# Attention and a block-quantised FFN on one core: up, down and output products cut into half jobs, placed by a table

## The chip, the cores and the metric

The kernel runs on one core of a Trainium2 chip. The metric is the device time of one launch in microseconds. PE is TensorE, DVE VectorE, ACT ScalarE, POOL GpSimd and SP SyncE.

## What is computed

Input x is 4 batches of 1024 tokens of width 128, fp32. xn is its layer norm, and the result is x plus attention of xn plus a gated FFN of xn.

```python
def _L0_attn_ref(inputs, Wq, bq, Wk, bk, Wv, bv, Wo, bo):      # 16 heads of 8
    q = split_heads(inputs @ Wq + bq)                           # k, v alike
    bias = alibi_slopes(H)[:, None, None] * rel                 # rel = key position
    scores = jnp.einsum('bhqd,bhkd->bhqk', q, k) * scale + bias[None]
    attn = jax.nn.softmax(scores, axis=-1)
    ctx = jnp.einsum('bhqk,bhkd->bhqd', attn, v)
    return ctx @ Wo + bo
...
def fp4_linear(x, w):                                           # blocks of 16 on a 4-bit grid
    return jnp.einsum('bsk,nk->bsn', fp4_quant_dequant(x), fp4_quant_dequant(w))
gate = fp4_linear(x, w_gate)                                    # 128 -> 352
y = fp4_linear(x, w_up)
h = jax.nn.silu(gate) * y
return fp4_linear(h, w_down)                                    # 352 -> 128
...
xn = _layernorm(x, axis=-1)
x = x + _L0_attn_ref(xn, ...) + _L0_ffn_ref(xn, ...)
```

## The kernel before

**Attention, in units.** Four heads at a time (a quad), half of the queries (512) at a time, the work goes by blocks of 128 keys: a unit U has four score products (keys x 512 queries, one for each head, L955), four exponentials (L630) and one value product of four heads in column tiles (L966, eight passes), which adds up over the eight units of a half in the bank pv. There are 256 units (NU), 8 to a half and 64 to a batch. The value product of unit U - 1 stands at the end of unit U. The softmax needs each row's maximum first. For that the scores are made once more with queries as rows: a chunk is 128 queries x 1024 keys of one head, in two products (L936), and DVE takes its maximum (L811). Sixteen chunks make a half. Chunks run ahead of the scores by LEAD, which is 22: 22 are done before unit 0, then two in each unit. On PE the products of a chunk and the scores are issued in turn and work on different halves of the rows, a pair at a time. When a half's sixteen maxima are there, DVE writes them in two bf16 parts (L816, L817, called the maximum parts here), PE turns them (job "turn", L944), ACT copies them (L636), and SP writes them to DRAM and back into a row of the queries' operand (L379, L382), two units before the half's first score.

**Jobs.** Everything else is a job that is put into a unit by a formula of its number (`extras`, L99): the FFN goes by pairs of token tiles (16 pairs, one in every 15 units): xT (transposes of the quantised input), gate (two halves, a product of 352 columns each), up (both halves, four passes, L989), hT (two, three transposes each, L997), down (both halves, twelve passes, L1005). The projections of a group of four token tiles are xnT, q, k, v. pvT transposes a finished half of pv (L1016) after ACT has copied it (L667), and DVE divides by the row sums (L841, L842). ctxT and wo (L1029) make the output of a group. All jobs of a unit stand in its middle: on PE after its first chunk and two scores, on ACT after two exponentials, on DVE before the unit's second maximum.

**Two rings of banks.** The first three banks of `low` are a ring for scores and for the jobs that ACT empties (xT, gate, hT, xnT, q, k, v, turn, ctxT, the weights' gT, uT, dT); the two slots of `mx`, two banks each, are a ring for chunks and for what DVE empties (up, down, pvT, wo, bvo). The n-th use of a ring waits until use n - 3 (n - 2 in mx) has been read (`free_bank`, `free_slot`). Each engine works in the order of its own code; semaphores count the uses.

**The quantiser.** After up, DVE multiplies gate and up to hid (L826), takes block maxima of hid and of the next pair's xn (L784, L787), scales and reciprocals (L795 to L798), POOL multiplies (L477, L479), DVE masks exponents (the powers, L804), and POOL rounds by an addition and a subtraction (L489 to L508), from which hT and the next xT are made. POOL also makes the gate's swish (L551), the norm of later groups and the three bf16 parts of q and k.

Of the kernel before, what the change touches and what calls it, by code (L numbers as in the profile page):

```python
# [13 lines left out]
P = 128  # L14
# [3 lines left out]
I = 352  # L18
# [85 lines left out]
def extras(U):  # L104

    out = []
    p, f = divmod(U - ffn_unit(0), ffn_unit(1) - ffn_unit(0))
    if 0 <= p < NP:
        out += {0: [("xT", p)], 1: [("gate", p, 0)], 2: [("gate", p, 1)], 4: [("up", p)], 12: [("hT", p, 0)],
                13: [("hT", p, 1)], 14: [("down", p)]}.get(f, [])  # L110
    for g in range(2, NG):
        if 0 <= U - group_unit(g) < 4:
            out.append((("xnT", "q", "k", "v")[U - group_unit(g)], g))
    out += [("turn", m) for m in range(LEAD // 16, HALVES) if turn_unit(m) == U]
    m, f = U // KT - 1, U % KT
    if m >= 0:
        out += [("pvT", m)] * (f == 2)
        if m // 2 % QUADS == QUADS - 1:
            out += {4: [("ctxT", m // 8 * 2 + m % 2)], 5: [("wo", m // 8 * 2 + m % 2)]}.get(f, [])
    out += {0: [("bvo",)], 7: [("gT",)], 8: [("uT",)], 9: [("dT",)]}.get(U, [])  # L120
    return out


IN_DVE_RING = ("up", "down", "pvT", "wo", "bvo")


def rings():
# [16 lines left out]
    for U in range(NU + KT):  # L144
        for i in range(2):
            if LEAD + 2 * U + i < CHUNKS:
                to_dve("max", LEAD + 2 * U + i)
            for j in (2 * i, 2 * i + 1):
                if U < NU:
                    to_act("exp", U, j)  # L150
            for job in extras(U) if i == 0 else ():
                (to_dve if job[0] in IN_DVE_RING else to_act)(*job)
# [6 lines left out]
def attn_ffn(nc, x, wq, bq, wk, bk, wv, bv, wo, bo, wg, wu, wd, out):  # L159
    with ExitStack() as ctx:  # L160
# [145 lines left out]
        def _(sp):  # L306
# [78 lines left out]
            def store(hb):  # L385
                g, i = hb, hb % 2
                sp.wait_ge(mx_free, MX["wo", hb] + 1)
# [14 lines left out]
            for U in range(NU + KT):  # L402
                for m in range(LEAD // 16, HALVES):
                    if turn_unit(m) + 1 == U:
                        max_rows(m)
                for g in range(2, NG):
                    if group_unit(g) + 8 == U:
                        parts_to_dram(g)
                for b in range(1, B):
                    for quad in range(QUADS):  # L410
                        if max(group_unit(2 * b + 1) + 9, (b - 1) * QUADS * UNITS + (quad + 1) * UNITS + 1) == U:
                            gather(b, quad)
                for job in extras(U - 1):
                    if job[0] == "wo":
# [6 lines left out]
        def _(pool):  # L421
# [136 lines left out]
            for U in range(NU):  # L558
                b, u = divmod(U, QUADS * UNITS)
                if u == 2:  # L560
                    add_bias(b)
                for g in range(2, NG):
                    if U == group_unit(g) - 2:
                        normalize(g)
                    if U == group_unit(g) + 2:
                        three_parts(g, 0, "q")
                    if U == group_unit(g) + 3:
                        three_parts(g, 1, "k")
                for p in range(NP):
                    if U == ffn_unit(p) + 3:  # L570
                        swish(p)
                    if U == ffn_unit(p) + 5:
                        scale_to_grid(p + 1)
                    if U == ffn_unit(p) + 7:
                        round_on_grid(p + 1)
# [3 lines left out]
        def _(act):  # L579
# [57 lines left out]

            std(0)
# [18 lines left out]
            for U in range(NU + KT):  # L657
# [10 lines left out]
                for job in extras(U):  # L668
                    kind, p = job[0], job[1] if len(job) > 1 else 0
                    if kind == "xT":  # L670
                        full("xT", p)
                        if p:
                            act.wait_ge(mx_full, MX["up", p - 1] + 1)
                        nc.scalar.copy(xqT[:], bank("xT", p)[:, 0:PW]).then_inc(st_free, 1)
                    elif kind == "gate":
                        t = job[2]
                        full("gate", p, t)
                        if p:
                            act.wait_ge(mx_free, MX["up", p - 1] + 1)
                        nc.scalar.activation(tanh_s[:, t * I:(t + 1) * I], bank("gate", p, t)[:, 0:I], ACT.Tanh, scale=0.5)  # L680
                        nc.scalar.copy(gate_s[:, t * I:(t + 1) * I], bank("gate", p, t)[:, 0:I]).then_inc(st_free, 1)  # L681
                    elif kind == "hT":
                        t = job[2]
                        full("hT", p, t)
                        if p:
                            act.wait_ge(mx_full, MX["down", p - 1] + 1)
# [418 lines left out]
```

## Time and profile before

| what | value |
|---|---|
| median of 3 runs | 901.21 us (895.38 to 918.01) |
| the profiled execution | 894.07 us |
| its span | 892.3 us |
| PE, DVE, ACT, POOL busy | 87%, 83%, 71%, 39% of the span |
| maxima on DVE (512) | 611.6 us |
| exponentials on ACT (1024) | 552.0 us |
| DMA | 35 GB/s over the span |

The span is from the first to the last instruction of the program; the profiled execution's own time lies 1.8 us above it. In a timeline row stand the start, the duration, the engine, the line, the operation, the tiles (written <- read) with partitions x elements, the number of instructions, and in brackets how long the engine had been idle and for whom it waited. The sum of busy times of one engine says how much work it has; who sets the length of a unit is read from the order of starts.

### The profile page before, as it was taken

To read this page: it belongs to the slowest core of one execution; us is meant where nothing else is said; L and a number is where in the kernel's file an instruction comes from. 1 tells how busy PE (TensorE), PEld (TensorE's weight loads), DVE (VectorE), ACT (ScalarE), POOL (GpSimd) and SP (SyncE) were. 2 spreads that over 40 slices of the span, in tenths; PEclk is the share of its full clock that TensorE was granted. 3 is DMA by queue.
4 is the path that set the end of the run, shared out by engine and by line. 5 is a ranking of instruction groups with operands and counts; after the bars stand their busy time and mean duration, and the time that the engine had idled before them with its cause. 6 is when DMAs were issued, how large, how long until landed. Compare 5 with 4: busy or idle time off the path is not lost.

```text
span 892.3 us, 13552 instructions
## 1 busy us (share of the span) xinstructions
PE 772.9 (87%) x4939; PEld 225.7 (25%) x4939; DVE 741.1 (83%) x878; ACT 633.0 (71%) x1262; POOL 349.3 (39%) x271
## 2 busy tenths in 40 slices
PE   3279989898989989897989989898989898979896
PEld 2012223221223323231323323222213231313222
DVE  7898898889888888978898888989897989898920
ACT  4106878777777878776877778777777687767775
POOL 7272172624226373715053553615152505141320
PEclk9557999999999999999999999999999999999999
DMA  5900020131001020320102020310102000000000
GB/s 156 256 13 2 1 72 3 52 92 36 3 13 37 13 72 2 101 44 1 37 2 49 13 73 1 107 37 1 37 2 49 13 3 1 2 1 2 2 1 24
DMA packets 32826, 31.83 MB, mean 36 GB/s; under 512 B 4344, under 2 KB 26552, under 8 KB 32760
## 3 DMA queue, kind: packets, MB, share of 16 engines
q1 hardware_dynamic: 32760, 30.96, 12.8%
q8 instruction: 40, 0.66, 0.3%
q14 instruction: 26, 0.21, 0.1%
HBM read 15.91 MB, written 15.04 MB: 35 GB/s over the span
## 4 chain that ended last, share of the span: by engine, by line
PE 58%; DVE 27%; ACT 8%; issue 4%; POOL 2%; DMA 1%; SPq 0%; ACTq 0%; DVEq 0%; POOLq 0%
PE low L966 22%; DVE neg_max L811 19%; PE mx L936 18%; ACT probs L630 6%; PE low L955 5%; PE mx L1005 3%; PE mx L989 3%; PE low L983 2%; DVE am L784 1%; DVE mb L804 1%; PE low L922 1%; ACT pv_s L667 1%; PE low L997 1%; DVE hid L826 1%; DVE inv L798 1%
## 5 line engine op out<-in xcount | busy, mean ns | idle before, releaser
L811 DVE TENSOR_REDUCE neg_max<-mx 128x1 f32<-128x1024 f32 x512 | 611.6, 1221 | 91.6 <-PE mx L936 80.2
L630 ACT ACTIVATE probs<-low 128x512 f32<-128x512 f32 x1024 | 552.0, 603 | 182.1 <-PE low L955 180.4
L936 PE MATMUL mx<-k_op,q_op 51*128 51x512 bf16 x1024 | 318.5, 398 | 55.9 <-DVE neg_max L811 33.4
L955 PE MATMUL low<-q_op,k_op 53*128 53x512 bf16 x1024 | 329.0, 389 | 8.0 <-ACT probs L630 2.5
L966 PE MATMUL low<-probs,v_op 128*32 128x512 f32 x2048 | 277.4, 614 | 7.1 <-ACT pv_s L667 5.9
L551 POOL TENSOR_SCALAR tanh_s<-tanh_s 128x704 f32<-128x704 f32 x16 | 31.7, 1982 | 313.7 <-ACT gate_s L681 313.7
L936 PEld LDWEIGHTS mx<-k_op,q_op 51*128 51x128 bf16 x1024 | 62.6, 95 | 358.5 <-DVE neg_max L811 197.2
L955 PEld LDWEIGHTS low<-q_op,k_op 53*128 53x128 bf16 x1024 | 68.5, 94 | 76.5 <-ACT probs L630 63.8
L489 POOL TENSOR_SCALAR mb<-mb 128x960 f32<-128x960 f32 (+2 forms) x17 | 58.8, 3456 | 39.6 <-DVE mb L804 37.9
L966 PEld LDWEIGHTS low<-probs,v_op 128*32 128x32 f32 x2048 | 40.5, 108 | 89.9 <-issue 46.1
L477 POOL TENSOR_TENSOR zb<-hid,inv 128x704 f32<-128x704 f32 x16 | 22.2, 1387 | 97.7 <-DVEq L799 97.7
L491 POOL TENSOR_TENSOR zb<-zb,mb 128x960 f32<-128x960 f32 (+2 forms) x17 | 38.2, 2247 | 1.3
L490 POOL TENSOR_TENSOR zb<-zb,mb 128x960 f32<-128x960 f32 (+2 forms) x17 | 38.2, 2244 | 1.4
L636 ACT COPY max_t<-low 32x128 bf16<-32x128 bf16 x32 | 8.1, 254 | 39.1 <-PE low L944 39.0
L983 PE MATMUL low<-gT_s,xqT 128*128 128x352 f32 x64 | 27.5, 511 | 0.2
L552 POOL TENSOR_TENSOR gate_s<-tanh_s,gate_s 128x704 f32<-128x704 f32 x16 | 27.0, 1686 | 1.3
L944 PE MATMUL low<-ident_b,neg_parts 128*32 128x128 bf16 x32 | 7.2, 224 | 22.4 <-DVE neg_parts L817 19.4
L1005 PE MATMUL mx<-dT_s,hqT 128*128 128x128 f32 (+1 forms) x192 | 25.7, 283 | 0.0
L1016 PE MATMUL mx<-ident,pv_s 128*128 128x128 f32 x128 | 20.2, 280 | 5.0 <-DVE neg_max L811 3.9
L1005 PEld LDWEIGHTS mx<-dT_s,hqT 128*128 128x128 f32 (+1 forms) x192 | 22.6, 191 | 6.8 <-DVE neg_max L811 4.7
L989 PE MATMUL mx<-uT_s,xqT 128*128 128x352 f32 x64 | 23.2, 485 | 0.0
L501 POOL TENSOR_TENSOR hq<-zb,sc 128x704 f32<-128x704 f32 x16 | 22.3, 1392 | 1.3
(120 smaller groups left out, 522.3 us busy)
## 6 DMA issues: line engine op xcount, KB each, us to landing
q_op<-q_rows SPq DMA_DIRECT2D x32, 192.0 KB, 3.8
k_op<-k_rows SPq DMA_DIRECT2D x32, 192.0 KB, 4.7
q_rows<-qp SPq DMA_DIRECT2D x8, 384.0 KB, 2.6
k_rows<-kp SPq DMA_DIRECT2D x8, 384.0 KB, 3.2
x_s<-in_L_attn_inputs_dram SPq DMA_DIRECT2D x8, 256.0 KB, 3.7
q_rows<-qp SPq DMA_DIRECT2D x8, 256.0 KB, 3.1
k_rows<-kp SPq DMA_DIRECT2D x8, 256.0 KB, 3.1
out_dram<-o_s SPq DMA_DIRECT2D x8, 256.0 KB, 2.3
```

The costliest lines, as they stand in the source:

```text
L489: link(nc.gpsimd.tensor_scalar(m, m, 1.0, ROUND, ALU.max, ALU.mult))
L490: link(nc.gpsimd.tensor_tensor(z, z, m, ALU.add))
L491: link(nc.gpsimd.tensor_tensor(z, z, m, ALU.subtract))
L551: link(nc.gpsimd.tensor_scalar(tanh_s[:], tanh_s[:], 1.0, None, ALU.add))
L630: nc.scalar.activation(probs[U % 3][:, 2 * g + x, :], bank("exp", U, j), ACT.Exp).then_inc(st_free, 1)
L811: nc.vector.tensor_reduce(to, slot("max", pos)[:], AX.X, ALU.max, negate=True).then_inc(mx_free, 1)
L936: ins = nc.tensor.matmul(slot("max", pos)[:, 512 * kh:512 * kh + 512], q, k, start=True, stop=True)
L955: nc.tensor.matmul(bank("exp", U, j), k_op[quad][r, g, kt * P:(kt + 1) * P], q_op[quad][r, g, half * HALF:(half + 1) * HALF], start=True, ...
L966: ins = nc.tensor.matmul(pv[32 * hh:32 * hh + 32, :], v_op[b % 2][:, kt, 4 * quad + hh, :], probs[U % 3][:, hh, :], start=(kt == 0), stop= ...
L983: nc.tensor.matmul(bank("gate", p, t)[:, 0:I], xqT[:, t * P:(t + 1) * P], gT_s[:], start=True, stop=True).then_inc(st_full, 1)
L989: ins = nc.tensor.matmul(slot("up", p)[:, 512 * t:512 * t + I], xqT[:, t * P:(t + 1) * P], uT_s[:], start=True, stop=True)
L1005: ins = nc.tensor.matmul(slot("down", p)[:, t * P:(t + 1) * P], hqT[t][0:n, c * P:(c + 1) * P], dT_s[0:n, c * P:(c + 1) * P], start=(c == ...
```

## The change

Up, down and wo, which DVE empties, are cut into two jobs of half the size. `extras` and the formulas of unit numbers go; `plan` builds a table AT at build time. A unit may hold one job in its middle (gate, q, k, v, the weights' transposes and bvo) and one at its end (all others); a job whose place is taken moves to the next unit. At the end means: on PE behind the value product, which now stands right after the unit's last score, on ACT after the fourth exponential, on DVE after the second maximum. ACT's copy of pv moves from behind the second exponential to behind the first. The block maxima are taken inside the second up half's job, the scales after the next unit's first maximum, the reciprocal after its second. LEAD is 23, so a half's last maximum and its parts come one chunk sooner. The gate weights' transposes move from units 7 to 9 to units 1 to 3, and the units of POOL's and SP's work are derived from the table.

```diff
-LEAD = 22
+LEAD = 23
...
-def ffn_unit(p):
-    return 10 + 15 * p
-
-
-def group_unit(g):
-    return 13 + 60 * (g // 2 - 1) + 15 * (g % 2)
+FFN_FIRST, FFN_STEP = 4, 15
+MIDDLE = ("gate", "q", "k", "v", "gT", "uT", "dT", "bvo")
+IN_DVE_RING = ("up", "down", "pvT", "wo", "bvo")
...
+def plan():
+
+    at, busy = {}, set()
+
+    def put(first, *job):
+        place = job[0] in MIDDLE
+        while (first, place) in busy:
+            first += 1
+        busy.add((first, place))
+        at[job] = first
+        return first
+
+    for U, job in enumerate(("bvo", "gT", "uT", "dT")):
+        put(U, job)
+    for m in range(HALVES):
+        if m >= LEAD // 16:
+            put(turn_unit(m), "turn", m)
+        put(KT * (m + 1) + 2, "pvT", m)
+    x_at = put(FFN_FIRST, "xT", 0)
+    for p in range(NP):
+        U = put(x_at + 1, "gate", p, 0)
+        U = put(U + 1, "gate", p, 1)
+        U = put(U + 2, "up", p, 0)
+        up = put(U + 1, "up", p, 1)
+        if p + 1 < NP:
+            x_at = put(max(FFN_FIRST + FFN_STEP * (p + 1), up + 7), "xT", p + 1)
+        U = put(up + 7, "hT", p, 0)
+        U = put(U + 1, "hT", p, 1)
+        U = put(U + 1, "down", p, 0)
+        put(U + 1, "down", p, 1)
...
+    for hb in range(2 * B):
+        U = put(at["pvT", hb // 2 * 8 + 6 + hb % 2] + 1, "ctxT", hb)
+        for i in range(2):
+            U = put(max(U, at["down", 2 * hb + 1, 1]) + 1, "wo", hb, i)
+    return at
...
-                for j in range(2):
+                for j in range(4):
                     exponential(U, j)
-                if U % KT == 1 and U > KT:
-                    m = U // KT - 1
-                    act.wait_ge(pv_done, U - 1)
-                    if m:
-                        act.wait_ge(mx_full, MX["pvT", m - 1] + 1)
-                    nc.scalar.copy(pv_s[:], pv).then_inc(pv_kept, 1)
...
+                    if j == 0 and U % KT == 1 and KT < U <= NU + 1:
+                        m = U // KT - 1
+                        act.wait_ge(pv_done, U - 1)
+                        if m:
+                            act.wait_ge(mx_full, MX["pvT", m - 1] + 1)
+                        nc.scalar.copy(pv_s[:], pv).then_inc(pv_kept, 1)
+                    for job in middle(U) if j == 1 else ():
+                        job_on_scalar(job)
+                for job in end(U):
+                    job_on_scalar(job)
...
+                    mark(nc.vector.scalar_tensor_tensor(hid[:, half], gate_s[:, half], 0.5, slot("up", p, t)[:, 0:I],
+                                                        ALU.mult, ALU.mult))
+                    settle()
                     dve.sem_inc(mx_free, 1)
+                    if t == 1:
+                        block_maxima(p + 1)
...
                     for p in range(NP):
-                        if U == ffn_unit(p) + 5 and i == 0:
-                            block_maxima(p + 1)
-                        if U == ffn_unit(p) + 5 and i == 1:
-                            block_scales(p + 1)
-                        if U == ffn_unit(p) + 7 and i == 0:
+                        if U == AT["up", p, 1] + 1:
+                            (block_scales if i == 0 else block_inverses)(p + 1)
+                        if U == AT["up", p, 1] + 3 and i == 0:
                             powers(p + 1)
+                for job in end(U):
+                    job_on_vector(job)
...
-                    for job in extras(U) if i == 0 else ():
+                    if 0 < U <= NU and i == 1:
+                        value_product(U - 1)
+                    for job in middle(U) if i == 0 else ():
                         job_on_array(job)
-                if 0 < U <= NU:
-                    value_product(U - 1)
+                for job in end(U):
+                    job_on_array(job)
```

On PE, near the down job of the sixth pair. mx<-k_op,q_op is half a chunk, low<-q_op,k_op a score, low<-probs,v_op the value product, mx<-dT_s,hqT down. Before, one unit and its neighbour's value product:

```order
L966 MATMUL low<-probs,v_op 32x512 x4
L936 MATMUL mx<-k_op,q_op 128x512
L955 MATMUL low<-q_op,k_op 128x512
L936 MATMUL mx<-k_op,q_op 128x512
L955 MATMUL low<-q_op,k_op 128x512
L1005 MATMUL mx<-dT_s,hqT 128x128 x6
L936 MATMUL mx<-k_op,q_op 128x512
L955 MATMUL low<-q_op,k_op 128x512
L936 MATMUL mx<-k_op,q_op 128x512
L955 MATMUL low<-q_op,k_op 128x512
L966 MATMUL low<-probs,v_op 32x512 x4
```

And now, from the end of one unit over the next:

```order
L1020 MATMUL low<-probs,v_op 32x512 x4
L1058 MATMUL mx<-dT_s,hqT 128x128 x3
L990 MATMUL mx<-k_op,q_op 128x512
L1009 MATMUL low<-q_op,k_op 128x512
L990 MATMUL mx<-k_op,q_op 128x512
L1009 MATMUL low<-q_op,k_op 128x512
L990 MATMUL mx<-k_op,q_op 128x512
L1009 MATMUL low<-q_op,k_op 128x512
L990 MATMUL mx<-k_op,q_op 128x512
L1009 MATMUL low<-q_op,k_op 128x512
L1020 MATMUL low<-probs,v_op 32x512 x4
L1069 MATMUL mx<-ident,pv_s 128x128 x4
```

Down has left the place between a unit's two chunks; half of it stands behind the value product, and so does pvT one unit later.

On DVE, from the up job of the second pair to the powers. neg_max<-mx is a chunk's maximum, hid the product of gate and up, am the block maxima, sc, scn and inv scales and reciprocal, mb the powers. Before:

```order
L826 SCALAR_TENSOR_TENSOR hid<-gate_s,mx 128x704
L811 TENSOR_REDUCE neg_max<-mx 128x1 x2
L784 TENSOR_REDUCE am<-hid 128x44
L787 TENSOR_REDUCE am<-xn_s 128x16
L811 TENSOR_REDUCE neg_max<-mx 128x1
L795 TENSOR_SCALAR sc<-am 128x60
L796 TENSOR_SCALAR scn<-am 128x60
L798 RECIPROCAL inv<-scn 128x60
L811 TENSOR_REDUCE neg_max<-mx 128x1 x3
L804 TENSOR_SCALAR mb<-zb 128x960
```

And now:

```order
L876 SCALAR_TENSOR_TENSOR hid<-gate_s,mx 128x352
L859 TENSOR_REDUCE neg_max<-mx 128x1 x2
L876 SCALAR_TENSOR_TENSOR hid<-gate_s,mx 128x352
L829 TENSOR_REDUCE am<-hid 128x44
L832 TENSOR_REDUCE am<-xn_s 128x16
L859 TENSOR_REDUCE neg_max<-mx 128x1
L840 TENSOR_SCALAR sc<-am 128x60
L841 TENSOR_SCALAR scn<-am 128x60
L859 TENSOR_REDUCE neg_max<-mx 128x1
L847 RECIPROCAL inv<-scn 128x60
```

The product comes in halves a unit apart, the block maxima stand directly behind the second one, and one maximum stands between the scales and the reciprocal.

## Rows read from the trace of the kernel before

**Rows 1.** The page, busy time of each engine (share of the span) x instructions.
```profile
PE 772.9 (87%) x4939; PEld 225.7 (25%) x4939; DVE 741.1 (83%) x878; ACT 633.0 (71%) x1262; POOL 349.3 (39%) x271
```
**Rows 2.** The page's costliest group: busy, mean ns | idle before, releaser.
```profile
L811 DVE TENSOR_REDUCE neg_max<-mx 128x1 f32<-128x1024 f32 x512 | 611.6, 1221 | 91.6 <-PE mx L936 80.2
```
**Rows 3.** Timeline of PE over a unit without a job: start, duration, what.
```profile
129.02 1.06 PE L966 MATMUL low<-probs,v_op 128*32 128x512 f32 x8
...
131.17 0.39 PE L955 MATMUL low<-q_op,k_op 53*128 53x512 bf16 x1
131.48 1.06 PE L966 MATMUL low<-probs,v_op 128*32 128x512 f32 x8
```
**Rows 4.** Timeline of ACT and of DVE in the same unit.
```profile
130.51 2.06 ACT L630 ACTIVATE probs<-low 128x512 f32<-128x512 f32 x4 [0.39 <-PE low L955]
...
128.20 4.81 DVE L811 TENSOR_REDUCE neg_max<-mx 128x1 f32<-128x1024 f32 x4 [0.31 <-PE mx L936]
```
**Rows 5.** Timeline of PE, a unit with hT in its middle.
```profile
136.34 0.55 PE L997 MATMUL low<-ident,hq 128*128 128x128 f32 x3
136.82 0.39 PE L936 MATMUL mx<-k_op,q_op 51*128 51x512 bf16 x1
```
**Rows 6.** Timeline of PE, a unit with down.
```profile
142.24 1.60 PE L1005 MATMUL mx<-dT_s,hqT 128*128 128x128 f32 x12
143.78 0.39 PE L936 MATMUL mx<-k_op,q_op 51*128 51x512 bf16 x1
```
**Rows 7.** Timeline of PE, the copy of pv and the unit with pvT.
```profile
223.43 1.07 PE L966 MATMUL low<-probs,v_op 128*32 128x512 f32 x8 [0.58 <-ACT pv_s L667]
...
224.96 0.66 PE L1016 MATMUL mx<-ident,pv_s 128*128 128x128 f32 x4
226.35 0.39 PE L936 MATMUL mx<-k_op,q_op 51*128 51x512 bf16 x1 [0.73 <-DVE neg_max L811]
```
**Rows 8.** Timeline of PE, up and q behind each other, then k.
```profile
302.24 1.45 PE L989 MATMUL mx<-uT_s,xqT 128*128 128x352 f32 x4
303.53 1.02 PE L922 MATMUL low<-xnT_s,wq_s 128*128 128x512 f32 x2
...
306.99 1.12 PE L922 MATMUL low<-xnT_s,wk_s 128*128 128x512 f32 x2
308.05 0.39 PE L936 MATMUL mx<-k_op,q_op 51*128 51x512 bf16 x1
```
**Rows 9.** Timeline of DVE after the up of the third pair.
```profile
207.57 0.89 DVE L826 SCALAR_TENSOR_TENSOR hid<-gate_s,mx 128x704 f32<-128x704 f32 x1 [0.22 <-PE mx L989]
...
211.30 0.88 DVE L784 TENSOR_REDUCE am<-hid 128x44 f32<-128x704 f32 x1
...
212.42 1.22 DVE L811 TENSOR_REDUCE neg_max<-mx 128x1 f32<-128x1024 f32 x1
...
214.54 3.49 DVE L811 TENSOR_REDUCE neg_max<-mx 128x1 f32<-128x1024 f32 x3
217.95 0.65 DVE L804 TENSOR_SCALAR mb<-zb 128x960 int32<-128x960 int32 x1
```
**Rows 10.** Timeline of PE, four units behind that up.
```profile
219.79 0.39 PE L936 MATMUL mx<-k_op,q_op 51*128 51x512 bf16 x1 [0.69 <-DVE neg_max L811]
```
**Rows 11.** Timeline of PE, value products 0 and 254 (x256 in all).
```profile
72.24 1.08 PE L966 MATMUL low<-probs,v_op 128*32 128x512 f32 x4
...
881.81 1.06 PE L966 MATMUL low<-probs,v_op 128*32 128x512 f32 x8
```
**Rows 12.** Timeline of DVE and POOL where both work on SBUF.
```profile
417.70 2.19 DVE L817 TENSOR_TENSOR neg_parts<-neg_max,neg_parts 128x16 bf16<-128x16 f32 x1
...
417.66 2.21 POOL L490 TENSOR_TENSOR zb<-zb,mb 128x960 f32<-128x960 f32 x1
```
**Rows 13.** Timeline of SP's queue and of PE, at the start of a half.
```profile
190.41 1.01 SPq L382 DMA_DIRECT2D q_op<-m_rows  x2
...
193.51 0.39 PE L955 MATMUL low<-q_op,k_op 53*128 53x512 bf16 x1
```

More of the change, by code:

```diff
@@ L101 @@
 HEAD = ((1, 0), (1, 1), (0, 0), (0, 1))
[L104 to L121, printed above, removed]
@@ L124, with norm_unit, parts_unit @@
-IN_DVE_RING = ("up", "down", "pvT", "wo", "bvo")
+def norm_unit(b):
+    return 1 if b == 1 else 60 * b - 59
+def parts_unit(g):
+    return 60 * (g // 2 - 1) + 16 + 15 * (g % 2)
+def plan():
[25 more added lines that the diff above has]
+        put(U + 1, "down", p, 1)
+    for b in range(1, B):
+        for g in (2 * b, 2 * b + 1):
+            U = norm_unit(b) + 1 + 8 * (g % 2)
+            for name in ("xnT", "q", "k"):
+                U = put(U + 1, name, g)
+            assert U < parts_unit(g)
+            put(max(U, QUADS * UNITS * (b - 1) + 2) + 1, "v", g)
+    for hb in range(2 * B):
[3 more added lines that the diff above has]
+    return at
@@ L127, in rings, with middle, end @@
+AT = plan()
+JOBS = {}
+for _job, _unit in AT.items():
+    JOBS.setdefault(_unit, []).append(_job)
+def middle(U):
+    return [job for job in JOBS.get(U, ()) if job[0] in MIDDLE]
+def end(U):
+    return [job for job in JOBS.get(U, ()) if job[0] not in MIDDLE]
 def rings():
@@ L143, in rings, with to_ring @@
             to_act("turn", 0)
-    for U in range(NU + KT):
+    def to_ring(job):
+        (to_dve if job[0] in IN_DVE_RING else to_act)(*job)
+    for U in range(NU + 2 * KT):
         for i in range(2):
@@ L401, in _ @@
             max_rows(0)
[L402 to L405, printed above, removed]
+            for U in range(NU + 2 * KT):
+                for job in JOBS.get(U - 1, ()):
+                    if job[0] == "turn":
+                        max_rows(job[1])
                 for g in range(2, NG):
-                    if group_unit(g) + 8 == U:
+                    if parts_unit(g) + 4 == U:
                         parts_to_dram(g)
@@ L655, in _ @@
             keep_turn(0)
[L657 removed]
+            for U in range(NU + 2 * KT):
                 if 3 <= U < NU:
                     act.wait_ge(pv_done, U - 2)
[L660 removed]
+                for j in range(4):
                     exponential(U, j)
[L662 to L711 removed]
@@ L872, in _ @@
             block_scales(0)
+            block_inverses(0)
             for pos in range(LEAD):
@@ L876, in _ @@
                 reduce_chunk(pos)
-            for U in range(NU + KT):
+            for U in range(NU + 2 * KT):
                 for i in range(2):
                     pos = LEAD + 2 * U + i
-                    if i == 1:
-                        for job in extras(U):
-                            job_on_vector(job)
+                    for job in middle(U) if i == 1 else ():
+                        job_on_vector(job)
                     if pos < CHUNKS:
@@ L1065, in _ @@
                     turn(0)
-            for U in range(NU + KT):
+            for U in range(NU + 2 * KT):
                 for i in range(2):
```

161 lines of the change are left out of this document (92 added, 69 removed).

## The prediction

> **What bounds the kernel now.** I read the page's busy line first: PE is busy 87% of the span, DVE 83%, ACT 71%, POOL 39% [rows 1]. The costliest group, the row maxima on DVE, is 611.6 us [rows 2], so DVE is near the end-setter without being it. The averages don't say what ends a unit, so I went to the timeline of one unit without any job. From one value product to the next is 131.48 - 129.02 = 2.46 us [rows 3]. In those 2.46 us the fourth score stands at 131.17, 1.15 us after the unit's first pair (1.00 us behind the value product's start, at 130.02). Low has three banks, so this score takes the bank of the unit's first score, which ACT frees when its first exponential (start 130.51, four of them in 2.06 us [rows 4], so 0.49 apart and about 0.6 long) is done. Then 0.31 us later the value product starts, and it holds PE for 1.00 us. So a clean unit is a loop PE, ACT, PE: 0.49 + 0.60 + 0.06 + 0.31 + 1.00 = 2.46. DVE needs two maxima, 1.14 apart when nothing is missing (four in 4.81 us with 0.1 idle, [rows 4]), 2.28: it has 0.18 to spare in a unit, and a second chunk may come 0.3 us late before it moves the fourth score.
>
> Jobs cost the rest. Value product 0 starts at 72.24 and value product 254 at 881.81 [rows 11]: 809.6 us for 254 units, of which 254 x 2.46 = 624.8 are clean and **184.7 us are jobs and what they cause**. That number is what the change acts on.
>
> Prices of before, each a unit's length less 2.46. A job in the middle with a bank of low shifts the ring by one bank, so the fourth score waits for the second exponential: +0.49, and the job's own PE time (0.48 for three transposes, 136.34 to 136.82 [rows 5]) is hidden in it. A job in the middle in a slot of mx is dearer: the unit's second chunk then needs the slot of the first, which is read until 1.86 us into the unit (0.64 to the maximum's start, 1.22 for it). After pvT it comes at 226.35, 1.92 into a unit that began at 224.43, 1.00 behind its value product [rows 7]: +0.99. Down holds PE longer, 142.24 to 143.78 [rows 6], +1.15; up, four products in 1.29 us [rows 8], +1.05. The copy of pv after the second exponential holds the value product by 0.65 (223.43 in rows 7, waiting for ACT's pv_s).
>
> **What the change does to each.** Behind the value product a job meets other conditions. Its bank was freed long ago, so no exponential is waited for; its PE time is no longer hidden and is paid in full. In mx the next unit's first chunk needs the slot of this unit's second chunk, whose maximum ends 1.14 after the first one's, 3.00 into the unit and 0.54 behind a clean unit's end: a floor of 0.60 under every mx job that follows a clean unit.
> The join is not shown: no row has a full-array fp32 job directly behind the value product. Nearest rows: chunk pairs follow it 0.09 later than its passes alone need, and the transposes of rows 5 give back the same 0.09; between two full-array fp32 products there is no gap (302.24 + 4 x 0.32 = 303.53 [rows 8]). So the job starts 0 to 0.09 us sooner than the next pair would. I take 0, as every change of kind in the rows has the gap, and keep 0.1 for the range. The Trainium skill bears on this (TensorEngine Tiling (Array Packing), Key Properties): changing the tiling mode, not just the tile, drains TensorE. The value product runs in 32-column tiles, a job in the full array, so by that rule the gap is there; without it the sum below would be some 15 us lower. No row shows this join.
>
> Prices after, per piece:
> - xT, 16: two transposes, 0.31 + a little for ACT's copy: 0.35. 5.6 us
> - hT, 32: 0.42 + 0.04: 0.46. 14.7 us
> - ctxT and xnT, 13: 0.53 + 0.09 (ACT copies 0.6 before the next exponential): 0.62. 8.1 us
> - turn, 31: one small transpose and its copy: 0.20. 6.2 us
> - pvT, 31, and half wo, 13: the slot's floor, 0.60. 26.4 us
> - half up, 32: 2 x 0.32 + 0.09 = 0.73, less a little: 0.72. 23.0 us
> - half down, 31: 6 x 0.11 + 0.09 = 0.77. 23.9 us
> - pv's copy, 31, now behind the first exponential, 0.49 sooner: 0.65 - 0.49 = 0.17. 4.8 us, as a few lie under another job
> - in the middle as before: 35 with one bank x 0.49 = 17.2; 18 projections at 0.67 to 0.70 (k holds PE 306.99 to 308.05 [rows 8]): 12.2 us
>
> Sum 142.1 us. Halving alone is a loss: up was 1.05 and is 1.44, down 1.15 and now 1.54, 16 of each, +12.5. The gains are pvT (0.99 to 0.60, -12), turn (0.49 to 0.20, -9) and pv's copy (about -8 where it stood alone).
>
> To this comes **DVE's debt**, not removed but moved. After up, DVE has the product (0.89), two block maxima (211.30 to 212.42, 1.12 more than none), scales and reciprocal (to 214.54, 0.99) and later the powers (0.65), against 0.18 spare a unit [rows 9]; the second chunks of the units behind it come late, as at 219.79 after 0.69 us idle for DVE [rows 10]. In the regular stretch of the new table (16 units for a pair: xT; gate and hT; gate and hT; down; pvT; down; up; turn; up; three without a job; pvT; two without; turn) I walked the units by the four rules above. With parts, halves and powers in their places the second up is followed by units that are 0.50, 0.62, 0.03 and 0.36 too long and a pvT dearer by 0.13, and before it 0.33 and after it 0.08 go to the maximum parts: 2.05 us a pair, 16 pairs 32.8, less about 5 where projections, wo or ctxT stand in these units and would have waited anyway: 27.5. Splitting scales and reciprocal round a maximum is in these numbers.
> DVE and POOL also meet: a 16-element subtraction took 2.19 us (417.70) while POOL's 2.21 us addition ran (417.66) [rows 12]. In the regular stretch the parts of every second turn fall about 7.8 us behind the powers, near the end of POOL's second addition, for some 0.4 us, 12 times: 5 us.
>
> Total after: 142.1 + 27.5 + 5 = 174.6 against 184.7: -10.1. One more leading chunk costs a maximum, +1.2, weights transposed at U 1 to 3 at a lower clock +0.5, down and wo behind the last value product +0.2. Net -8.2. The profiled execution took 894.07 us for a span of 892.3 (1.8 around it), so its like would be 885.9. The median of the runs shown is 901.21, 0.8% above it, the lowest 895.38; the runs of a kernel differ by more than the profiled one shows, so I say 887 for a median.
>
> **The rivals.**
> 1. No gap behind the value product, and the debt better covered: 0.09 to 0.1 on about 155 jobs, -15, net -23: 871. For it: nothing drains between full-array jobs, and passes follow each other at 0.11. Against: every change of kind in the rows has its gap. Faster by over 2%.
> 2. POOL's additions catch the maximum parts (slower than before). The place is the cast and subtraction in the unit ahead of each second turn; the price is up to 2.2 us each [rows 12] against my 0.4, so up to 1.8 x 13 = 23 us, and the turn behind it waits too: 886 + 23 = 909. It decides if the cast starts in the first third of an addition, 1.5 us sooner than I place it. For it: the new table is periodic, so a hit repeats in every pair. Against: my placing, and that such delays already cost before.
> 3. The maxima arrive late. The turn now starts 1.9 us later, two units ahead of the scores that need its rows. From the copy's end the chain takes 2.4 us to its last issue; in one place of before the scores started 2.09 us after that issue ended, unhindered (190.41 + 1.01, 193.51 [rows 13]). So 0.65 + 2.4 + 2.1 = 5.15 us at most are needed and 5.1 or more are there: about 0; were it a microsecond short each time, 31 us and 917.
> 4. The split does what it says but the DVE debt is as large as its whole extra work, 7 us a pair less the spare 2.9, double mine: +33 less what jobs cover, half: 901.
>
> **How the numbers follow.** Forecast 0.55 (880 to 893); rival 1 0.29; rival 2 0.05; rival 3 0.04; rival 4 0.07. About 2% is what a measurement of this kernel can tell from no change. Faster by over 2% needs under some 879: rival 1 and the forecast's lower edge, 0.33. Slower by over 2%: rivals 2 and 3 at full price, 0.09. Within: 0.58. The range reaches from rival 1 (868) to rival 4 and most of 2 (905).
>
> **What would show it.** Right: clean units still 2.46; a unit with half a down at its end about 3.2, with pvT 3.06; value products 0 to 254 about 800 us apart; idle of the chunk's products for DVE smaller after pvT, present behind the second up; first transpose of an hT about 1.0 us behind the value product's start. Wrong: that start at 0.9 (rival 1); casts of 1 us or more, regularly (2); scores at a half's start waiting for a DMA (3); units of over 3.2 without jobs after up (4).

## The result and the profile after

| kernel | median | runs | beside it, before |
|---|---|---|---|
| changed | 1028.59 us (1014.70 to 1035.55) | 4 | 898.30 us (893.39 to 918.01) |

The ratio is 1.1385, 95% interval 1.1246 to 1.1524: the changed kernel is 13.9% slower. Medians here are over all executions, ratios over the faster ones alone, as some executions of several kernels, the traced one of the changed kernel among them, are some per cent longer at a lower mean clock. The forecast was 887 us, the range 868 to 905. The profiled execution took 1031.83 us for a span of 1029.9.

The page of the changed kernel, busy time by engine, then the granted clock in 40 slices, then its costliest groups:

```profile
PE 941.4 (91%) x4939; PEld 301.5 (29%) x4939; DVE 746.4 (72%) x918; ACT 640.2 (62%) x1262; POOL 346.6 (34%) x271
...
PEclk9555579999999999999998999799999999979999
...
L859 DVE TENSOR_REDUCE neg_max<-mx 128x1 f32<-128x1024 f32 x512 | 610.0, 1218 | 196.9 <-PE mx L990 196.5
...
L990 PE MATMUL mx<-k_op,q_op 51*128 51x512 bf16 x1024 | 366.9, 408 | 45.7 <-DVE neg_max L859 26.4
L1009 PE MATMUL low<-q_op,k_op 53*128 53x512 bf16 x1024 | 360.2, 396 | 13.4 <-ACT probs L672 9.2
```

PE has exactly as many instructions as before, 4939, yet is busy 941.4 us against 772.9 [rows 1]; DVE's and ACT's busy times are within 1.2% of before. DVE's maxima now wait 196.9 us, nearly all of it for PE, against 91.6 [rows 2]. So PE has become the bound, and not by more work. One unit without a job shows how, start and duration, on PE:

```profile
211.50 1.06 PE L1020 MATMUL low<-probs,v_op 128*32 128x512 f32 x8
212.49 0.39 PE L990 MATMUL mx<-k_op,q_op 51*128 51x512 bf16 x1
212.72 0.38 PE L1009 MATMUL low<-q_op,k_op 53*128 53x512 bf16 x1
212.94 0.55 PE L990 MATMUL mx<-k_op,q_op 51*128 51x512 bf16 x2
213.16 0.54 PE L1009 MATMUL low<-q_op,k_op 53*128 53x512 bf16 x2
213.54 0.38 PE L990 MATMUL mx<-k_op,q_op 51*128 51x512 bf16 x1
213.85 0.39 PE L1009 MATMUL low<-q_op,k_op 53*128 53x512 bf16 x1
214.16 0.64 PE L1020 MATMUL low<-probs,v_op 128*32 128x512 f32 x4
```

The first two pairs of a unit before the change (the unit of rows 3):

```profile
130.02 0.39 PE L936 MATMUL mx<-k_op,q_op 51*128 51x512 bf16 x1
130.02 0.39 PE L955 MATMUL low<-q_op,k_op 53*128 53x512 bf16 x1
130.25 0.38 PE L936 MATMUL mx<-k_op,q_op 51*128 51x512 bf16 x1
130.25 0.38 PE L955 MATMUL low<-q_op,k_op 53*128 53x512 bf16 x1
```

Before, a chunk's product and a score start in the same instant, and the next pair 0.23 us later. After, the unit's first four products start 0.22 to 0.23 us behind one another, and so do the later ones but where the unit passes from one half of the rows to the other (in the single records a chunk's product at 213.10 and a score at 213.16): what was done by two is done one by one. The order of instructions on PE in this unit has not changed. What has changed is which rows of the array they use. `chunk` gives the chunk at position pos the rows x = pos % 2, and `score` takes its rows from HEAD, (1, 0), (1, 1), (0, 0), (0, 1): first two scores on half 1, then two on half 0. Unit U has the chunks LEAD + 2U and LEAD + 2U + 1. With LEAD 22 the first of them lies on half 0, beside scores on half 1, and the second on half 1, beside scores on half 0. With LEAD 23 chunk and score of a pair lie on the same half. The unit went from 2.46 to 214.16 - 211.50 = 2.66 us; a unit with an xT behind its first value product and a gate half in the middle takes 4.10 (3.32 in the run with LEAD 22 below), and with an hT in xT's place 4.21 (3.44): 0.78 more, where a unit without a job loses 0.21. PE's spare time in the unit, in which it waited for ACT, is gone there.

Where the clock is low it is dearer still. Engine sums by stretch, busy us and (instructions), then PEclk, first before, then after:

```profile
72.00:78.00 6.00, 6.00 (x30) 1.09 (x30) 3.92 (x4) 3.08 (x6) 1.54 (x4) 0.53 0.00 0
78.00:300.00 222.00, 203.16 (x1355) 60.02 (x1351) 191.98 (x209) 172.01 (x346) 84.75 (x63) 1.00 0.11 32
```
```profile
75.00:138.00 63.00, 62.75 (x177) 16.31 (x176) 23.55 (x22) 28.22 (x52) 4.67 (x3) 0.50 0.00 1
138.00:300.00 162.00, 156.62 (x883) 50.77 (x882) 128.20 (x150) 112.97 (x224) 60.56 (x43) 0.99 0.12 36
```

Before, PE is full from 72 us and its clock is at the upper level from 78. After, PE is full from 75 to 138 us, 62.75 of 63, and the granted clock is 0.50 (1.2 GHz) throughout: units take 5.9 to 8.6 us there. Worked out from the granted clocks (0.962 and 0.918 of the span, with two levels), the half-clock time is 68 us before and 169 after.

Of the 1017.87 - 889.89 = 128 us by which value product 254 is later here than in the trace with LEAD 22 (experiment 1), 6.2 lie before value product 0, 36.6 between it and value product 16, and 85.2 behind that. In these three stretches the clock was at the lower level for 53, 63 and 48 us here and for 47, 1 and 21 us there. An estimate from these times, if the lower level does half the work of the upper: 95 us more at the lower level cost some 48 of the 128 us, and the products one by one at the upper level the other 80. So the larger part of the loss needs no lower clock.

### The profile page after: what moved, and what is told of

Read it like the earlier page. It is cut to its first block, busy times and chain, and to the rows that moved or that the text cites. A ratio compares the mean times of both kernels' runs of the same rounds, so it can differ in the third digit from the quotient of the medians.

```text
span 1029.9 us, 13671 instructions
## 1 busy us (share of the span) xinstructions
PE 941.4 (91%) x4939; PEld 301.5 (29%) x4939; DVE 746.4 (72%) x918; ACT 640.2 (62%) x1262; POOL 346.6 (34%) x271
## 4 chain that ended last, share of the span: by engine, by line
PE 71%; DVE 17%; ACT 4%; issue 4%; DMA 2%; POOL 1%; SPq 1%; ACTq 0%; DVEq 0%; POOLq 0%
PE low L1020 22%; PE mx L990 18%; PE low L1009 16%; DVE neg_max L859 12%; ACT probs L672 3%; PE low L1037 3%; PE mx L1058 3%; PE mx L1043 2%; PE mx L1069 2%; PE low L976 2%; PE low L1050 1%; DVE neg_parts L864 1%; ACT pv_s L752 1%; PE low L972 1%; DVE hid L876 1%
## 5 line engine op out<-in xcount | busy, mean ns | idle before, releaser
L859 DVE TENSOR_REDUCE neg_max<-mx 128x1 f32<-128x1024 f32 x512 | 610.0, 1218 | 196.9 <-PE mx L990 196.5
L672 ACT ACTIVATE probs<-low 128x512 f32<-128x512 f32 x1024 | 543.5, 603 | 256.5 <-PE low L1009 253.1
L990 PE MATMUL mx<-k_op,q_op 51*128 51x512 bf16 x1024 | 366.9, 408 | 45.7 <-DVE neg_max L859 26.4
L1009 PE MATMUL low<-q_op,k_op 53*128 53x512 bf16 x1024 | 360.2, 396 | 13.4 <-ACT probs L672 9.2
L1020 PE MATMUL low<-probs,v_op 128*32 128x512 f32 x2048 | 289.1, 638 | 2.0
L990 PEld LDWEIGHTS mx<-k_op,q_op 51*128 51x128 bf16 x1024 | 94.9, 97 | 280.8 <-DVE neg_max L859 131.3
L1009 PEld LDWEIGHTS low<-q_op,k_op 53*128 53x128 bf16 x1024 | 95.1, 96 | 142.3 <-ACT probs L672 92.7
L887 DVE TENSOR_TENSOR x_s<-mx,x_s 128x128 f32<-128x128 f32 x32 | 9.3, 292 | 27.7 <-PE mx L1058 27.7
L876 DVE SCALAR_TENSOR_TENSOR hid<-gate_s,mx 128x352 f32<-128x352 f32 x32 | 16.7, 521 | 16.9 <-PE mx L1043 16.9
L1043 PE MATMUL mx<-uT_s,xqT 128*128 128x352 f32 x64 | 28.6, 529 | 0.0
L699 ACT COPY hqT<-low 128x384 f32<-128x384 f32 x32 | 15.3, 479 | 20.1 <-PE low L1050 19.9
```

Source lines behind the costliest of these rows:

```text
L672: nc.scalar.activation(probs[U % 3][:, 2 * g + x, :], bank("exp", U, j), ACT.Exp).then_inc(st_free, 1)
L859: nc.vector.tensor_reduce(to, slot("max", pos)[:], AX.X, ALU.max, negate=True).then_inc(mx_free, 1)
L990: ins = nc.tensor.matmul(slot("max", pos)[:, 512 * kh:512 * kh + 512], q, k, start=True, stop=True)
L1009: nc.tensor.matmul(bank("exp", U, j), k_op[quad][r, g, kt * P:(kt + 1) * P], q_op[quad][r, g, half * HALF:(half + 1) * HALF], start=True, ...
L1020: ins = nc.tensor.matmul(pv[32 * hh:32 * hh + 32, :], v_op[b % 2][:, kt, 4 * quad + hh, :], probs[U % 3][:, hh, :], start=(kt == 0), stop= ...
L1043: nc.tensor.matmul(slot("up", p, t)[:, 0:I], xqT[:, t * P:(t + 1) * P], uT_s[:], start=True, stop=True).then_inc(mx_full, 1)
```

## The experiments

**1. The changed kernel with LEAD 22.**
```diff
-LEAD = 23
+LEAD = 22
```


> The changed kernel with LEAD = 22 again, nothing else. Theory A (row halves): a chunk's half of the rows follows its position's parity, so LEAD = 23 put chunk and scores on the same half and their products one behind the other; with 22 the pairs start together again, a clean unit is 2.46 us instead of 2.67, a gate unit 2.95 plus its end job, and the time is 875 to 895 us. Theory B (jobs behind the value product are dear in themselves): pairs or not, the time stays above 980 us. Theory C (the lead's length or the turn's place): also 875 to 895 here, told from A by the next run.

Measured: 907.26 us (903.28 to 909.18) against 903.01, ratio 1.0073 (1.0043 to 1.0103). One number takes away 121 us. It is still above the 875 to 895 expected; what stands in that difference is the subject of experiments 5 and 9. PE in a unit without a job, start and duration:

```profile
160.04 1.07 PE L1020 MATMUL low<-probs,v_op 128*32 128x512 f32 x8
161.04 0.39 PE L990 MATMUL mx<-k_op,q_op 51*128 51x512 bf16 x1
161.04 0.39 PE L1009 MATMUL low<-q_op,k_op 53*128 53x512 bf16 x1
...
162.18 0.39 PE L1009 MATMUL low<-q_op,k_op 53*128 53x512 bf16 x1
162.50 1.06 PE L1020 MATMUL low<-probs,v_op 128*32 128x512 f32 x8
```

Pairs again, and 2.46 us. The rest of the change costs 0.7% and doesn't gain.

**2. The changed kernel, LEAD 23 kept, scores on the other rows first.** If the row halves are the cause, and not the one chunk more ahead, the order of the scores must mend it too.
```diff
-HEAD = ((1, 0), (1, 1), (0, 0), (0, 1))
+HEAD = ((0, 0), (0, 1), (1, 0), (1, 1))
```


> The changed kernel with LEAD = 23 and the order of the four heads in a unit turned round, so that scores and chunks again use different halves of the rows. Theory A: as the run with LEAD = 22, 875 to 895 us, at most 2 us apart from it. Theory C (it is the lead itself): stays at 1010 to 1035 us. Theory B: above 980 us.

Measured: 909.87 us, ratio 1.0093 (1.0061 to 1.0125), the same as with LEAD 22. The leading chunk is innocent: LEAD 23 costs nothing when the scores change sides with it.

**3 and 4. The kernel before with each of the two edits alone.**
```diff
-LEAD = 22
+LEAD = 23
```


> The kernel before with LEAD = 23 alone. Theory A: the products are issued one behind the other, a clean unit becomes 2.67 us or more, gate and hT units lose their cover (0.9 us more of PE in a unit), and the clock may rise later: 980 to 1030 us. Theory B: 893 to 900 us, as the lead costs one maximum.

and, LEAD 22 kept,
```diff
-HEAD = ((1, 0), (1, 1), (0, 0), (0, 1))
+HEAD = ((0, 0), (0, 1), (1, 0), (1, 1))
```


> The kernel before with LEAD = 22 and the order of the heads turned round: the same half of the rows for chunk and score, with no change of lead. Theory A: within 1% of the kernel before with LEAD = 23, 980 to 1030 us. Theory B and C: 893 to 900 us.

Measured: 1059.28 us (1030.52 to 1061.76) against 903.01, and 1017.91 us (1010.96 to 1033.50), ratio 1.1278 (1.1214 to 1.1342). The loss comes without the jobs' new table: even the quickest execution of the third is 14% above the kernel before. The two were expected within 1% of each other and are 4% apart; their granted clocks differ too (below), and why is open. The fourth one's maxima group, then PE in one of its units without a job:

```profile
L811 DVE TENSOR_REDUCE neg_max<-mx 128x1 f32<-128x1024 f32 x512 | 618.3, 1222 | 218.1 <-PE mx L936 212.2
```
```profile
184.32 1.06 PE L966 MATMUL low<-probs,v_op 128*32 128x512 f32 x8
185.32 0.56 PE L936 MATMUL mx<-k_op,q_op 51*128 51x512 bf16 x2
185.55 0.55 PE L955 MATMUL low<-q_op,k_op 53*128 53x512 bf16 x2
185.77 0.55 PE L936 MATMUL mx<-k_op,q_op 51*128 51x512 bf16 x2
...
186.99 0.64 PE L966 MATMUL low<-probs,v_op 128*32 128x512 f32 x4
```

Again 0.22 apart and 2.67 us. The four cases with the mean granted clock of their traced executions:

| | pairs on two halves | pairs on one half |
|---|---|---|
| kernel before | LEAD 22: 0.962 | LEAD 23: 0.911; other scores first: 0.925 |
| changed kernel | LEAD 22: 0.961; LEAD 23, other scores first: 0.960 | LEAD 23: 0.918 |

The weights' transposes in the first units are not what lowers the clock: experiments 1 and 2 have them there and keep 0.96, experiments 3 and 4 don't and lose it. How much of the lower clock belongs to the pairing is less clear than the table looks. The three traces on the right are of executions 17 to 28 us longer than their kernel's quickest. Over all executions the clock was 0.909 to 0.934 in the changed kernel, 0.907 to 0.937 in the third and 0.925 to 0.955 in the fourth; the kernel before, run beside the two, had 0.950 to 0.961 in twelve of its fourteen, and 0.930 in the other two (916 and 919 us), neither of them traced. Three of the fourth's four executions had 0.947 to 0.955, hardly less than the kernel before, and took 1011 to 1018 us. So the products one by one cost over 100 us with the clock nearly the same, and what the clock adds on top differs from one execution to the next.

Where the clock falls differs too. The fourth's rises at 78 us, as before the change, and falls at 460, just behind a wait of 1.48 us of PE for a maximum; it comes back at 504. In the trace of the kernel before it falls at 408.7 behind the same wait of 1.48 us and is back after 3.4 us. Two stretches of the fourth (PE, PEld, DVE, ACT and POOL busy, then PEclk):

```profile
460.00:480.00 20.00, 20.00 (x73) 4.07 (x75) 11.56 (x13) 9.42 (x18) 10.27 (x6) 0.50 0.00 1
480.00:500.00 20.00, 20.00 (x66) 4.25 (x58) 8.60 (x9) 9.64 (x18) 0.00 (x0) 0.50 0.16 40
```

PE is busy without a break, at 0.50, for 40 us and more; the third shows the same from 151 to 209 us, the changed kernel from 75 to 138.

**5. What is left of the change's loss: POOL's order.** With LEAD 22 the changed kernel's PE stands still once for 6.28 us. PE there, then POOL:

```profile
472.52 1.09 PE L966 MATMUL low<-ident,xn_s 128*128 128x128 f32 x4 [6.28 <-POOL xn_s L570]
```
```profile
466.17 2.20 POOL L534 TENSOR_TENSOR zb<-zb,mb 128x960 f32<-128x960 f32 x1
468.45 1.39 POOL L544 TENSOR_TENSOR hq<-zb,sc 128x704 f32<-128x704 f32 x1
469.79 0.62 POOL L551 TENSOR_TENSOR xq<-zb,sc 128x256 f32<-128x256 f32 x1
470.63 3.46 POOL L570 TENSOR_SCALAR xn_s<-x_s,rstd,nmr 128x128 f32<-128x128 f32 x8 [0.22 <-POOL xq L551]
```

The norm of groups 6 and 7 stands at unit 121, behind a rounding of nearly 10 us, and xnT of group 6 needs it at unit 123. Another gap of 2.71 us (at 590.48) is an xT behind the parts of group 7. Both were moved, with LEAD 22:
```diff
+    if g == 7:
+        return 147
...
-                    if U == norm_unit(g // 2):
+                    if U == (norm_unit(g // 2) if g < 6 else 115):
```


> The changed kernel with LEAD = 22, POOL's norm of the last two groups in unit 115 instead of 121 and the three parts of the last group in unit 147 instead of 151. Theory A2 (what is left over the kernel before is mainly POOL work that stands behind a rounding): the 6.3 us gap of PE before the transposes of xn and the 2.7 us gap before those of xq go, 9 to 12 us less than with LEAD = 22 alone: 894 to 899 us on a chip where the kernel before takes 903, ratio 0.992 to 0.999. Theory B2 (the half jobs' price): the gaps close but the time moves by under 3 us.

Measured: 897.56 us (895.38 to 899.24) against 903.59, ratio 0.9974 (0.9950 to 0.9998). Both gaps are gone, and between value products 0 and 254 the time fell from 817.8 to 808.7 us. So those two places cost 9 us, as expected; the table as such, with the halves in it, is worth nothing (809.6 before).

**6. The kernel before with the copy of pv behind the first exponential.**
```diff
                 for j in range(2):
                     exponential(U, j)
-                if U % KT == 1 and U > KT:
+                    if j == 0 and U % KT == 1 and U > KT:
```


> The kernel before with ACT's copy of pv behind the first exponential instead of the second, alone. Working of the prediction: 0.49 us less where the copy stands alone in its unit, about 18 of 31 units: 8 us less, ratio 0.990 to 0.993. Rival: the wait is taken over by the maxima on DVE, ratio 0.998 to 1.002.

Measured: 905.38 us (896.20 to 1164.87), ratio 1.0020 (0.9983 to 1.0056): no gain. The longest execution, at a mean clock of 0.558, was not traced. Where the copy stands alone, its unit fell from 3.11 to 2.62 us, the 0.49 of the prediction. Where the same unit has a job of low's ring in its middle, it rose from 3.10 to 3.44: the second exponential comes later behind the copy, and with the job's bank shift the fourth score needs just that one's bank (read from the order of the code). That pvT in the next unit takes a part back, as it is bound by DVE's slot, is argued and not measured alone.

**7 and 8. The kernel before with pvT, turn and wo behind the value product**, all jobs whole, up and down still in the middle; the seventh with the sixth's copy of pv, the eighth without it.
```diff
+END = ('pvT', 'turn', 'wo')
...
                 if 0 < U <= NU:
                     value_product(U - 1)
+                for job in end(U):
+                    job_on_array(job)
```


> The kernel before with the pv copy moved and pvT, turn and wo, whole, behind the value product; up, down and all else stay whole in the middle, LEAD 22, old unit numbers. By the prices of the prediction and of the run with LEAD = 22: pvT -12, turn -9 to -14, pv copy -8, wo -1, some back where two jobs shared a unit: 25 to 33 us less, 868 to 880 us, ratio 0.96 to 0.975. Rival (DVE is next and takes it back): ratio 0.98 to 0.99.

> As the run before, but with the pv copy where it was: 8 us slower than that one by the prediction's price; 2 us or less if DVE takes it back.

Measured: 884.68 us (881.31 to 1400.08; the longest, at a mean clock of 1.00, was not traced and is not explained), ratio 0.9811 (0.9763 to 0.9860), and 882.93 us (880.53 to 884.79), ratio 0.9801 (0.9752 to 0.9850). The move to the end is the part of the change that gains, about 2% by the medians and 12 us between value products 0 and 254 by the traces (809.6 to 797.7). It is less than the 25 to 33 us expected for the seventh, and the copy of pv, priced at 8 us, makes no difference between the two. The three jobs were moved together, so their shares are not measured apart. The join behind the value product in the eighth, PE:

```profile
224.39 1.06 PE L986 MATMUL low<-probs,v_op 128*32 128x512 f32 x8
225.39 0.66 PE L1036 MATMUL mx<-ident,pv_s 128*128 128x128 f32 x4
...
227.45 1.06 PE L986 MATMUL low<-probs,v_op 128*32 128x512 f32 x8
```

A unit of 3.06 us with pvT, the floor of 0.60 that was worked out; the same unit took 3.45 before (its value products stood at 223.43 and 226.88).

**9. Halves against wholes**: the fifth with up and down put back as whole jobs into the middle.
```diff
-MIDDLE = ("gate", "q", "k", "v", "gT", "uT", "dT", "bvo")
+MIDDLE = ("up", "down", "gate", "q", "k", "v", "gT", "uT", "dT", "bvo")
...
-        U = put(U + 2, "up", p, 0)
-        up = put(U + 1, "up", p, 1)
+        up = put(U + 2, "up", p, 1)
```


> The changed kernel with LEAD 22 and POOL's norm and parts moved (the run before with these edits: 897.6 us), and up and down put back to whole jobs in the middle of a unit, as in the kernel before; its planner and its half output products stay. It tests the prediction's step that halving alone is a loss. By the prices (a half up 0.72 twice against 1.05, a half down 0.77 twice against 1.15, 16 of each) the halves cost 12.5 us: 885 us, and a unit with a whole up or down in the middle is 3.5 to 3.6 us long. Rival: the halves cost nothing net, because a whole job makes DVE late for the maxima behind it (0.9 and 1.1 us of DVE work in one place): 895 to 900. A third possibility, that the halves are a gain: over 900.

Measured: 881.25 us (880.50 to 882.74), ratio 0.9806 (0.9774 to 0.9837). Between value products 0 and 254 it is 795.5 us against the fifth's 808.7. Halving costs 13.2 us by the profiles and 16 by the medians, against 12.5 worked out. With the halves went the places of what follows them: the block maxima and the reciprocal stand again as in the kernel before, and later jobs moved by some units, so the 13.2 are the halves with all that hangs on them. The unit with a whole up is 3.50 us (its neighbours' value products at 191.34 and 194.84):

```profile
191.34 1.06 PE L1021 MATMUL low<-probs,v_op 128*32 128x512 f32 x8
...
192.93 1.45 PE L1045 MATMUL mx<-uT_s,xqT 128*128 128x352 f32 x4
194.31 0.39 PE L991 MATMUL mx<-k_op,q_op 51*128 51x512 bf16 x1
...
200.11 0.39 PE L991 MATMUL mx<-k_op,q_op 51*128 51x512 bf16 x1 [1.20 <-DVE neg_max L859]
```

The last row is DVE's debt, two units behind: 1.20 us of waiting for a maximum.

**10 and 11. The copy of pv sooner only where no job of low's ring stands beside it**, on the ninth and on the eighth.
```diff
-                    if j == 0 and U % KT == 1 and KT < U <= NU + 1:
+                    if j == any(job[0] not in IN_DVE_RING for job in middle(U)) and U % KT == 1 and KT < U <= NU + 1:
```


> The same, with the copy of pv behind the second exponential, as before, in those units whose middle has a job in one of low's banks, and behind the first one everywhere else. From the unit lengths of the earlier run the copy sooner gains 0.49 us where it stands alone and loses 0.33 where such a job stands beside it: some 12 such units, 3 to 4 us less than the whole-job kernel without this edit. Rival: the unit of pvT behind it takes everything back, no difference.

> The kernel before with pvT, turn and wo behind the value product (882.9 us in the earlier run), and the copy of pv behind the first exponential in the 18 of 31 units without a job in one of low's banks. 18 x 0.49 = 8.8 us less at most; the unit of pvT behind it is bound by DVE's slot and takes a part back (up to 0.6 in places of the earlier run): 875 to 880. Rival: pvT takes everything back, since its unit waits for the slot whenever its copy came: 882 to 884, no difference.

Measured: 879.77 us (876.39 to 880.87), ratio 0.9782 (0.9750 to 0.9813), and 881.47 us (878.54 to 884.71), ratio 0.9808 (0.9774 to 0.9843). By the profiles the stretch between value products 0 and 254 is 792.8 against 795.5 us, and 790.5 against 797.7: 3 and 7 us less. But in that stretch the clock was at the lower level for 5 us against 8, and for 5 against 15, so that (an estimate, at half the work) 2 of the 3 us and 5 of the 7 are the clock's. The medians are 1.5 us lower each, and the eleventh's ratio to the kernel before is no lower than the eighth's (0.9808 against 0.9801): a gain is not shown. The tenth has the lowest median found, not told apart from the ninth and the eleventh: the changed kernel's table with LEAD 22, up and down whole in the middle, POOL's norm sooner.

## Why the prediction was wrong

**The step that failed** is "One more leading chunk costs a maximum, +1.2". LEAD was priced as a count, at one maximum, and the clean unit was carried over as 2.46. But LEAD is also a phase: an odd number puts chunk and score of each pair on the same rows. Experiments 1 to 4 show it from all sides: in the kernel before, either edit alone breaks the pairing; in the changed kernel, which has LEAD 23, taking it back or adding the other edit restores it. The text ahead of the prediction already said that the two streams "work on different halves of the rows, a pair at a time"; I did not ask what keeps them there. The Trainium skill's page that the prediction drew on for the join (TensorEngine Tiling (Array Packing), Key Properties) also says that different tiles can run matmuls in parallel, and this case's traces agree and show the other side of it: together on two halves, 0.22 us apart on one. Read for the pairs too, that rule would have named the failure. None of the rivals named this mechanism, and a chance of 0.09 for slower by over 2% was too small for a kernel with a constant in it whose every use had not been followed.

**The rest, measured by experiment 1**, whose profiled time is 17 us above the sum (span 901.3 against 885.9 - 1.8 = 884.1), though the sum still has the 1.2 for the chunk that this run doesn't have. Unit lengths are distances of value products in its trace, at the upper clock level:

| term | price | measured |
|---|---|---|
| clean unit | 2.46 | 2.46 |
| hT at the end | 0.46 | 0.48 |
| xT | 0.35 | 0.37 |
| pvT | 0.60 | 0.59 |
| half up, half down | 0.72, 0.77 | 0.79, 0.86 |
| ctxT | 0.62 | 0.69 |
| turn | 0.20 | 0.03 |
| half wo, alone in its unit (9 of 13) | 0.60 | 0.63 to 2.33, mean 1.40 |
| DVE's lateness behind the second up half, up to and with the pvT | 1.64 | 1.63 |
| copy of pv alone | 0.17 | 0.15 to 0.18 |
| 16 units of the regular stretch | 48.6 | 48.9 to 49.2 |

Most unit prices held. Missed were POOL's two late places (9 us, experiment 5), which the prediction did not look for although the table moved the norm and the parts; and half wo, which the table puts into units in which DVE is late already, 7 us over its price in these nine units (PE's loads and products waited 9.7 us for DVE's addition behind it). DVE's subtraction met POOL's additions three times at 2.2 us, and thirteen more casts and subtractions took 0.5 to 1.1 us, where one alone takes 0.175: 12 us of DVE time over that in all, where 5 us of time had been put down. In the kernel before it was 9 us already, two subtractions of 2.19 among them. What of it reaches PE is not shown.

Of the prices of before, the turn's was read too low: 0.49, where a turn alone in its unit cost 0.95 in the median of ten (units of 2.95 to 4.94 us). PE waited 19.4 us in 13 places there for the maximum parts; in experiment 1, with the turn at the end, it was 2.7 us in 3. The median unit with a turn alone is 2.49 us there, but 3.07 in experiment 8, which has the turn at the end under the old unit numbers: the wait hangs on how far DVE is behind at that place, and not only on middle or end.

**Rival 1**, no gap behind the value product: wrong. A full-array job starts 1.00 us behind its start (225.39 - 224.39 above). A turn, which like the value product works in 32 columns, starts 0.88 behind it, in the changed kernel:

```profile
208.79 1.06 PE L1020 MATMUL low<-probs,v_op 128*32 128x512 f32 x8
209.67 0.22 PE L998 MATMUL low<-ident_b,neg_parts 128*32 128x128 bf16 x1
```

That 0.12 goes with the change of mode, and with it the trace agrees with what the prediction took from the Trainium skill (TensorEngine Tiling (Array Packing), Key Properties), that changing the tiling mode drains TensorE; the turn, which doesn't pay it, came at almost nothing. That the mode alone makes the 0.12 is not shown: the turn also differs in type and in size from the jobs it is compared with. **Rival 2**, POOL's additions: three hits of the full price in experiment 1, not one in each pair, and none in the changed kernel, where the longest after the start are a cast of 1.6 and a subtraction of 1.3 us. **Rival 3**, late maxima rows: in the changed kernel one weight load of a score waits for their DMA, 0.5 us in all, and none with LEAD 22. **Rival 4**, twice the debt: wrong by the regular stretch, 0.3 to 0.6 us above the walk. Its sign did appear: the unit without a job behind the second up half takes 3.58 us, over the 3.2 that were named. The debt of the walk comes nearly whole in this one unit, and the units behind it have little left, so the sign told of the place of the debt and not of its size.

"Halving alone is a loss, +12.5": right (13.2 in experiment 9). "The gains are pvT, turn and pv's copy": right for the first two with wo, taken together (experiment 8, 2%), wrong for the copy, which also delays the exponential behind it (experiment 6).

## What to carry to other kernels

A constant that shifts one stream against another is a phase before it is a count. Where products share the array by row halves, write down for each pair which half it uses, before and after; if PE's instruction count is the same and its busy time isn't, look whether starts that were equal now differ. And judge a change of many parts by its parts: here one lost 13%, one lost 13 us, one lost 9 us, one gained 2%, and only their sum was to be seen.

## What the runs showed of the hardware

- Two bf16 products of 512 columns on different halves of the rows start at the same time; on the same half the second starts 0.22 us later. At the lower clock level it is 0.40 to 0.43 us (starts at 545.89, 546.29, 546.72 and 547.14 in the changed kernel). In a unit without a job that costs 0.2 us and not the 0.9 of four such steps, since PE had waited for ACT there; with a gate half in the unit it is 0.78 (2.95 to 3.73 in experiments 3 and 4).
- A full PE row does not mean that the clock rises: 62.75 us of 63 busy at a granted clock of 0.50, with the products one by one. With pairs it was 0.53 in 72 to 78 us, the first stretch with a full row, and 1.00 behind it. All three traces with pairs on one half have such stretches of 41 to 63 us, at different places; in the traces with pairs on two halves the longest between the first rise and the last units is 6.8 us. Why is not shown, nor whether the longer executions of the kernel before have such stretches too.
- Short idle times of PE stand just ahead of falls of the granted clock to 0.50: in the trace of the kernel before 1.48 us ahead of 3.4 us at 0.50; in experiment 1 the 6.28 us ahead of (and partly in) 6.8 us.
- Behind the start of a value product of eight column-tiled passes a full-array product starts at 1.00 us, a row-tiled one too, and one in the same mode (a turn) at 0.88.
- The start of value product 0 moved by 3 us between traces of kernels that hardly differ up to there (71.8 to 75.0 in the kernel before and experiments 6, 7, 8 and 11; 72.1 to 75.2 in 1, 5, 9 and 10), which is more than some edits here are worth. The distance between two fixed value products leaves that out, but the granted clock between them has to be read beside it, as experiments 10 and 11 show.
